# Feed-forward of a decoder kernel: a table of slots for its steps, and the output bias inside the down-projection

## The reference

```
h = shift_token(x)                  # second half of the features comes from the token before
h = (h - mean) / sqrt(var + 1e-5) * lg + lb
a, g = split(h @ w1 + b1)           # 682 hidden features each
x = x + (a * gelu(g)) @ w2 + b2
```

## Time and profile before

| | us |
|---|---|
| median of 3 runs | 2443.47 (2440.64 to 2444.36) |
| the profiled execution, its own time | 2433.82 |
| its span, first to last instruction | 2432.2 |
| TensorE busy | 2219.9 (91%) |
| VectorE busy | 1686.4 (69%) |
| ScalarE busy | 1510.4 (62%) |
| GpSimd busy | 1363.0 (56%) |
| mean granted TensorE clock | 0.960 |

### The profile page before, as it was taken

How to read it: one execution, slowest core, us unless ns; L and a number is a source line. 1 busy time by engine, 2 the same in 40 slices (tenths; PEclk the granted TensorE clock), 3 DMA queues, 4 the chain that set the end, 5 groups by cost and what they waited for, 6 DMA issues and landing times. The chain is left out here.

```text
span 2432.2 us, 44944 instructions
## 1 busy us (share of the span) xinstructions
PE 2219.9 (91%) x14670; PEld 1571.3 (65%) x14760; DVE 1686.4 (69%) x3300; ACT 1510.4 (62%) x3450; POOL 1363.0 (56%) x1456
## 2 busy tenths in 40 slices
PE   2899999899999999799999996898899999978887
PEld 2444444444444543478888885787688888866776
DVE  1777888678888886577787774554687777855553
ACT  1277788678878887567776773333577766753332
POOL 3344665333334444767777664553677676646665
PEclk6699999899999999899999998999999999999998
DMA  8656677656676674110000001000100000001111
GB/s 181 95 106 128 130 145 143 123 137 150 146 159 160 150 149 137 49 47 1 2 1 1 1 6 57 10 9 1 38 1 2 1 2 1 1 22 36 44 39 35
DMA packets 92405, 161.06 MB, mean 66 GB/s; under 512 B 15848, under 2 KB 35032, under 8 KB 92184
## 3 DMA queue, kind: packets, MB, share of 16 engines
q1 hardware_dynamic: 89624, 149.80, 27.7%
q0 software_dynamic: 2560, 8.39, 1.0%
HBM read 93.54 MB, written 59.24 MB: 63 GB/s over the span
## 5 line engine op out<-in xcount | busy, mean ns | idle before, releaser
L923 DVE TENSOR_REDUCE MX<-PS 128x1 f32<-128x512 f32 x1024 | 642.9, 683 | 193.4 <-PE PS L525 183.1
L775 ACT ACTIVATE PT<-PS 128x512 f32<-128x512 f32 x1024 | 545.8, 600 | 132.0 <-PE PS L542 130.2
L525 PE MATMUL PS<-KS,QS 48*128 48x512 f32 x1024 | 355.6, 454 | 56.1 <-DMA KS<-hs 44.1
L542 PE MATMUL PS<-QS,KS 50*128 50x512 f32 x1024 | 385.1, 456 | 6.4 <-ACT PT L775 6.0
L542 PEld LDWEIGHTS PS<-QS,KS 50*128 50x128 f32 x1024 | 164.7, 187 | 269.5 <-issue 212.6
L558 PE MATMUL PS<-PT,VP 128*17 128x512 f32 x2048 | 272.8, 605 | 3.2 <-ACT OT L782 3.1
L628 PE MATMUL PS<-kT,qT 128*128 128x256 f32 (+1 forms) x1536 | 253.7, 306 | 1.6 <-DVE kT L1030 1.6
L525 PEld LDWEIGHTS PS<-KS,QS 48*128 48x128 f32 x1024 | 171.4, 192 | 119.5 <-issue 60.2
L1290 POOL TENSOR_TENSOR PB<-PB,RC 128x512 f32<-128x512 f32 (+1 forms) x256 | 235.0, 935 | 13.3 <-DVE RC L1048 13.3
L847 ACT ACTIVATE PB<-PS,NMf 128x256 f32<-128x256 f32 (+1 forms) x512 | 223.7, 450 | 24.6 <-DVE NMf L1039 22.6
L1272 POOL TENSOR_TENSOR RI<-RI,mhalf 128x8 f32<-128x8 f32 x128 | 213.9, 1671 | 10.7
(11 more groups left out here) (164 smaller groups left out, 5292.3 us busy)
## 6 DMA issues: line engine op xcount, KB each, us to landing
hs<-HL SPq DMA_DIRECT2D x64, 512.0 KB, 3.8
QS<-hs SPq DMA_DIRECT2D x192, 128.0 KB, 6.1
KS<-hs SPq DMA_DIRECT2D x192, 128.0 KB, 8.4
od<-OT SPq DMA_DIRECT2D x64, 256.0 KB, 5.9
OC<-od SPq DMA_DIRECT2D x32, 256.0 KB
cst<-rs SPq DMA_DIRECT2D x32, 256.0 KB
X<-x SPq DMA_DIRECT2D x8, 512.0 KB, 8.6
tab<-ctxT SPq DMA_DIRECT2D x8, 512.0 KB, 7.2
```

The lines of the kernel that those rows point to most:

```text
L525: pe.matmul(PS[:, bank, :], QS[rows, s, h // 2, qt * P:(qt + 1) * P], KS[rows, s, h // 2, :], start=True, stop=True).then_inc(fills("amax" ...
L542: pe.matmul(PS[:, bank, :], KS[rows, s, pair, kt * P:(kt + 1) * P], QS[rows, s, pair, :], start=True, stop=True).then_inc(fills("score", v ...
L775: act.activation(PT[:, kt % 2, 2 * i + half], PS[:, TURNS["score", vb, g, kt, half, i][0], :], ACT.Exp).then_inc(drains("score", vb, g, kt ...
L923: dve.tensor_reduce(MX[:, vb % 2, h // 8, qt, c:c + 1], PS[:, TURNS["amax", vb, h, qt][0], :], AX, ALU.max).then_inc(drains("amax", vb, h, ...
```

## The change

The order of a feed-forward step comes from a table, `MLP_ORDER`: in each of six slots it lists stages with a delay k, and step n issues the stage for batch n-k. A negative delay means that a stage is issued ahead of its batch. Stages that were whole are cut: `mstat` and `mnorm` into halves (two token tiles; half of the features), and the closing normalisation of layer 1 leaves `mdown` and becomes `fstat`, `frstd`, `fnorm`, `fstore`. The load of `Y` is a stage `yload` of its own.

The affine step of `mtr` moves from VectorE to ScalarE, ahead of its copy there:

```
-                dve.tensor_scalar(TT[:], PS[:, bank, :], cols[:, L, 12 + half:13 + half], cols[:, L, 14 + half:15 + half],
-                                  ALU.mult, ALU.add).then_inc(drains("mtr", L, b, half), 1)
+                act.activation(TT[:], PS[:, bank, :], ACT.Identity, bias=cols[:, L, 14 + half:15 + half],
+                               scale=cols[:, L, 12 + half:13 + half]).then_inc(drains("mtr", L, b, half), 1)
```

```
+            def mones(L):
+                dve.memset(U5[32:64], 1.0).then_inc(sem["u_ones"], 1)
...
             def mres(L, b):
-                if L == 0 and b == 0:
-                    pool.wait_ge(sem["b2_in"], 16)
-                pool.wait_ge(sem["hn"], NB * L + b + 1)
-                for i in range(4):
-                    m = pool.tensor_tensor(X[:, b, i], X[:, b, i], b2[:, L], ALU.add)
...
+                pool.wait_ge(sem["y_in"], 16 * (b + 1))
+                pool.wait_ge(sem["hn"], 2 * (NB * L + b) + 2)
                 for i in range(4):
+                    m = pool.tensor_tensor(X[:, b, i], X[:, b, i], Y[:, i], ALU.add)
+                m.then_inc(sem["x_res"], 1)
```

More of the change, by code:

```diff
@@ L156, in window_stages @@
         if n == NU + last - 1:
-            out += [("mstat", L, 0), ("mnorm", L, 0)]
+            out += [("mstat", L, 0, 0), ("mstat", L, 0, 1), ("mnorm", L, 0, 0), ("mnorm", L, 0, 1)]
         for place, (kind, part, k) in enumerate(WINDOW_ORDER):
@@ L218, in all_stages @@
     out += window_stages(0, 6 * [([], [])] + [([("split_mlp", 0, k)], [("split_mlp_lo", 0, k)]) for k in range(14)])
-    out += [("load_rot",), ("rot", 1), ("load_qkv", 1)]
-    out += mlp_stages(0, [[("split_qkv", 1, k)] for k in range(10)])
+    out += [("load_rot",), ("rot", 1)]
+    out += mlp_stages(0, [[("load_qkv", 1, 2 * k), ("load_qkv", 1, 2 * k + 1)] for k in range(5)] + [[("split_qkv", 1, k)] for k in range(10)])
     out += [("load_mlp", 1)]
@@ L666, in mtr @@
             def mtr(L, b, half):
-                pe.wait_ge(sem["hn"], NB * L + b + 1)
+                pe.wait_ge(sem["hn"], 2 * (NB * L + b) + half + 1)
                 bank = vacant(pe, "mtr", L, b, half)
@@ L880, in mup @@
                     act.wait_ge(*filled("mup", L, b, c))
-                    gate, bias, done = PS[64:P, 2 * q, :], cols[64:P, L, 10:11], sem["gate5"]
+                    gate, bias, done = PS[64:126, 2 * q, :], cols[64:126, L, 10:11], sem["gate5"]
                 if c >= 2:
@@ L1079, in mstat, with mnorm @@
                 m.then_inc(sem["mmean"], 1)
-            def mnorm(L, b):
+            def mnorm(L, b, half):
                 s = b % 2
                 T = ST[:, s]
-                dve.wait_ge(sem["mrstd"], NB * L + b + 1)
-                if b >= 2:
-                    dve.wait_ge(*filled("mtr", L, b - 2, 1))
-                for half in range(2):
-                    for i in range(4):
-                        m = dve.tensor_scalar(HN[:, s, i, half * P:(half + 1) * P], XS[:, s, i] if half else X[:, b, i, 0:P],
-                                              T[:, 64 + 2 * i:65 + 2 * i], T[:, 80 + i:81 + i], ALU.subtract, ALU.mult)
-                m.then_inc(sem["hn"], 1)
@@ L1103, in mup @@
+                for i in range(4):
+                    m = dve.tensor_scalar(HN[:, s, i, half * P:(half + 1) * P], XS[:, s, i] if half else X[:, b, i, 0:P],
+                                          T[:, 64 + 2 * i:65 + 2 * i], T[:, 80 + i:81 + i], ALU.subtract, ALU.mult)
+                m.then_inc(sem["hn"], 1)
             def mup(L, b, c):
-                q, n, w = c % 2, P if c < 5 else 64, c if c < 5 else 10
+                q, n, w = c % 2, P if c < 5 else 62, c if c < 5 else 10
                 if c < 5:
@@ new lines, in fstat @@
+            def fstat(L, b, half):
+                T, n = LNF[:, half], 2 * b + half
+                dve.wait_ge(*drained("mdown", L, b, 2 * half))
+                dve.wait_ge(*drained("mdown", L, b, 2 * half + 1))
+                for k in range(2):
+                    dve.bn_stats(T[:, 6 * k:6 * k + 6], X[:, b, 2 * half + k]).then_inc(sem["fstats"], 1)
+                for k in range(2):
+                    dve.wait_ge(sem["fstats"], 2 * n + k + 1)
+                    m = dve.bn_aggr(T[:, 32 + 2 * k:34 + 2 * k], T[:, 6 * k:6 * k + 6])
+                m.then_inc(sem["fmean"], 1)
@@ L1154, in vector, with fnorm @@
+            def fnorm(L, b, half):
+                T = LNF[:, half]
+                dve.wait_ge(sem["frstd"], 2 * b + half + 1)
+                for k in range(2):
+                    x = X[:, b, 2 * half + k]
+                    m = dve.tensor_scalar(x, x, T[:, 32 + 2 * k:33 + 2 * k], T[:, 48 + k:49 + k], ALU.subtract, ALU.mult)
+                m.then_inc(sem["fnormed"], 1)
             does = dict(begin=begin, split_w=split_w, tr_lo=tr_lo, amax=amax, fold=fold, inv=inv, res=res, stats=stats, norm_last=norm_last, window_consts=window_consts, rot=rotations, split_qkv=split_qkv, wzero=wzero,
@@ L1339, in gpsimd, with fstore @@
+            def fstore(L, b, half):
+                pool.wait_ge(sem["fnormed"], 2 * b + half + 1)
+                pool.dma_start(t["out"][b, 2 * half * P:2 * (half + 1) * P].rearrange("(t p) d -> p t d", p=P),
+                               X[:, b, 2 * half:2 * half + 2]).then_inc(sem["out"], 16)
             does = dict(begin=begin, split_w=split_w, mix=mix, mix_sum=mix_sum, heads_lo=heads_lo, ctx_lo=ctx_lo, maxrows=maxrows, scale=scale,
                         out_lo=out_lo, rstd=rstd, norm=norm, add_bo=add_bo,
-                        split_qkv=split_qkv, split_mlp_lo=split_mlp_lo, wpad=wpad, wrn=wrn, wqn=wqn, wscale=wscale, mstat=mstat, mtr=mtr, mup=mup, mres=mres, mdown=mdown,
+                        split_qkv=split_qkv, split_mlp_lo=split_mlp_lo, wpad=wpad, wrn=wrn, wqn=wqn, wscale=wscale, mstat=mstat, mtr=mtr, mup=mup, mres=mres, frstd=frstd, fstore=fstore,
@@ L1458, in load_qkv @@
                         heads_written(sp, NV - 1, 0, tile)
-                for k in range(10):
+                for k in range(10) if piece is None else (piece,):
                     _, _, raw, src = qkv_source(k)
```

171 lines of the change are left out of this document (67 added, 104 removed).

## The result

| | us |
|---|---|
| the changed kernel, median of 4 runs | 2365.23 (2364.60 to 2371.15) |
| the kernel before, beside it, 4 runs | 2443.91 (2440.64 to 2445.07) |
| ratio, 95% interval | 0.9686 (0.9667 to 0.9704) |
| the profiled execution after, own time; span | 2371.15; 2369.3 |

The change made the kernel faster by 78.7 us by the medians. By the two profiled executions the gain is 62.7.

A forecast was written before the change was run, and what follows sets the result against it. TensorE sets the pace in both feed-forward stretches but waits for `HN` and `HT` through orders, not loads. Savings 4.3 + 4.1 + 11.8 + 0.3 + 7.9 + 24.0 + 1.5 = 53.9 us, scaled to 54.1, gave 2389.5; range 2376 to 2408.

The forecast's parts named there:

- A stall of 1.2 is left: 167.1 + 7 x 1.2: Layer 1, steps 1 to 7: late tail stalls TensorE 1.2 us a step before the down-projection; 175.5 in all, 24.0 saved.
- Profiled time 2379.9; runs 2443.47 - 54.1 = 2389.4: Whole kernel: saving of 53.9 us taken from the profiled execution, scaled by 1.004 and taken from the runs' median.
- (a): Rival: VectorE is early enough, no tail stall in either layer; 3.0 + 8.4 us less, 2378; chance 0.13.
- Lead-in, 4.3 and 0.3 predicted: Before each layer's first product: affine pass on ScalarE, 0.69 us each, saves 4.3 in layer 0, 0.3 in layer 1.
- Layer 0, 15.9 predicted: Layer 0's steps: waits for `HN` and `HT` go, saving 4.1 us in step 0 and 11.8 in steps 1 to 7.
- in which TensorE never waits takes 24.0 us: Length of a feed-forward step without waits, from layer 0: transposes 25.29 us apart with a stall of 1.30.
- except where a weight split holds GpSimd in slot 5 (some 4 steps, 0.75 each): 3.0: Layer 0, steps 1 to 7: weight splits on GpSimd make the tail late, adding 3.0 us to 167.1.
- Layer 1, 31.9 predicted: Layer 1's steps: waits for `HN` and `HT` go, saving 7.9 us in step 0 and 24.0 in steps 1 to 7.
- (b): Rival: port holds add 2.8 us to the tail in each layer 1 step, step 28.0; +19.6, 2409; chance 0.18.
- (c): Rival: affine Identity pass between gate functions forces four ScalarE table loads a step; +21 us, 2410; chance 0.02.
- (d): Rival: slower than before, each VectorE two-port operation in layer 1 held a full 1.3 us pass; step 34.4, 2454; chance 0.03.
- (e): Rival: a queued wait, such as GpSimd's stores for the closing norm, hands back each gain; 2443 us; chance 0.02.

The follow-up runs named there:

- stat3: The changed kernel with both halves of the statistics of batch n+2 and the adds of `Y` moved to the end of slot 3; median 2364.19 us, ratio 0.9675.

## Why the prediction was right, and where it was wrong

The direction, the mechanism and the order of the parts were right: the waits for `HN` and `HT` were made by orders, and they went. The time was not, for two separate reasons. Of the steps of the sum, "A stall of 1.2 is left: 167.1 + 7 x 1.2" failed most, by its size: the stall is 0.52 to 0.57 in five steps and nothing in two. And the step from the profile to the median failed.

*The conversion from the profile to the median failed, 15.5 of the 24.3 us.* The prediction took "Profiled time 2379.9; runs 2443.47 - 54.1 = 2389.4", that is 9.6 between them. Measured, the median lies 5.9 below its profiled execution. Both are draws from a spread that the three runs of before (2440.64 to 2444.36) did not show, and that 50 more runs put at 29 us (whether the first chip has less of it, as its four runs of after within 6.6 us suggest, or this was chance, stays open). The range ended at 2376, "under (a) by 2"; it had no term for this. The other medians of the same or an equal feed-forward are 2376.45, 2385.46 and 2368.72: the first two lie in the range, the third 7.3 below it. Had the 9.6 held, the median would have been 2380.8, in the range with the sum as wrong as it is; had the sum been right and the draw the same, it would have been about 2375.5, just outside. So how far the median lies outside the range is for the larger part the luck of the draw.

(The rest of the 24.3 is 8.8: the 10.3 below and the 2.6 of "between", less the 3.9 of "ahead" and 0.2 of rounding and of what lies outside the span.)

*The sum was 10.3 too small.* What came true is nearer rival (a), fed fully, given 0.13: its 53.9 + 11.4 = 65.3 stands beside the measured 64.2. That is partly luck: a stall is left in layer 1, and the fed step is shorter than (a) had it. By the prediction's steps:

1. Lead-in, 4.3 and 0.3 predicted, 4.0 and 0.15 measured. The path was right (copies, `TT` single). Each affine pass took 0.78, not 0.69 (timelines of ScalarE and GpSimd):

```profile
1481.00 0.78 ACT L877 ACTIVATE TT<-PS,cols 128x512 f32<-128x512 f32 x1 [8.02 <-PE PS L672]
1481.81 0.62 ACT L882 CAST HT<-TT 128x512 fp32r<-128x512 f32 x1
1483.93 0.78 ACT L877 ACTIVATE TT<-PS,cols 128x512 f32<-128x512 f32 x1 [1.50 <-POOL HT L1319]
```
```profile
1482.57 1.26 POOL L1319 TENSOR_TENSOR HT<-TT,HT 128x512 fp32r<-128x512 f32 x1 [5.42 <-ACT HT L882]
1485.43 1.26 POOL L1319 TENSOR_TENSOR HT<-TT,HT 128x512 fp32r<-128x512 f32 x1 [1.60 <-ACT HT L882]
```

2. Layer 0, 15.9 predicted, 20.05 measured. Step 0 takes 19.05 (1486.80 to 1505.85) where 18.8 was put down, so nothing of the miss is there. Steps 1 to 7 take 165.70 where 170.1 was put down, for two reasons. The first is the fed step, "in which TensorE never waits takes 24.0 us". It takes 23.75, and step 7 takes 23.03 for 23.1. The 24.0 was one step of the earlier trace rows less its wait of 1.30, and such a step holds some 0.2 more behind the wait. This is worth 1.6 us in each layer. The second is "except where a weight split holds GpSimd in slot 5 (some 4 steps, 0.75 each): 3.0". A split beside the tail does lengthen its second pass (in four steps, to 1.13 or 1.82 for 0.74), but in layer 0, where no closing normalisation and no adds stand ahead, the tail has that much to spare. Steps 1 to 7 take only 0.17 more than fed ones in sum, and TensorE shows no idle time. One of the two longest (VectorE, then GpSimd), where the first down-projection follows at 1535.20:

```profile
1532.57 0.69 DVE L1137 TENSOR_TENSOR UR<-UR 32x512 fp32r<-32x512 f32 x1 [0.29 <-ACT UR L906]
1533.27 1.82 DVE L1138 SCALAR_TENSOR_TENSOR UR<-UR,cols 32x512 fp32r<-32x512 f32 x1
...
1533.26 1.28 POOL L1273 TENSOR_TENSOR WQ<-WQ 128x512 fp32r<-128x512 f32 x1 [3.90 <-ACT WQ L796]
```

3. Layer 1, 31.9 predicted, 38.0 measured. Step 0 takes 18.09 (2157.91 to 2176.00) for 18.4. Steps 1 to 7 take 169.7 for 175.5: 1.6 of it is the fed step, and the rest, 4.2, is "A stall of 1.2 is left: 167.1 + 7 x 1.2", the largest miss. It is there, before the first down-projection group as forecast, but at 0.52 to 0.57 in five steps, 2.7 for 8.4 (the steps of layer 1 are 1.5 longer in sum than the fed ones beyond these waits). Counted as the prediction did (the sixth up-projection ends at 2249.25, 5.6 before the need), the product starts at 1.89 for 2.3, the copies are done at 3.9 for 4.5, the tail at 6.0 for 6.8: each link was put a little too long, and a wait that is the difference of two long sums doubles by it. Steps 1 and 7 have none at all. The bound given, "none", was right as a bound. The cause was right too: the prediction charged the statistics ahead of the product and the blocked tail, and the wait goes when either is taken away.

4. The end, 1.5 predicted, 2.0 in "close". The 2.2 less of idle time (5.38 for 7.59) came as forecast; of the 0.7 that was to be lost behind it, some 0.1 shows. "Between" gained 2.6 that no step had.

The other rivals: (b) is out, as the tail pays 0.67 and not 2.8 for its neighbour in the steps with the wait (0.95 in step 7, which has none). (c) is out, with one table load in a layer as before (groups by line of the changed kernel):

```profile
L896 ACT ACT_TABLE_LOAD x2 | 2.6, 1283 | 0.0
```

By the Trainium skill, ScalarE: Activation LUTs, Table sets, identity is in every set; the trace agrees. (d) needed every `HN` half held for a whole pass. The second half of `HN` did get longer, 0.562 for 0.335 in the mean of an operation (the first 0.498 for 0.594), but either half is early enough. (e) is out, as no gain was handed back.

On the rule of the shared port (the Trainium skill, Advanced Engine Details and Errata, Mode Summary), the trace agrees for `HN` and goes further than that section: the tail's passes, which have two tensors as sources, are longer beside GpSimd's adds too, 0.98 to 1.28 for 0.68 and 1.12 for 0.74. The rule was weighed in the prediction as a danger to the change (a 1.3 at the product's neighbours), and what it is worth here is the 0.5 us in a step that moving GpSimd's adds by two slots gives back.

## What to carry to other kernels

Where no queue is full and TensorE still waits, change the order first: the table brought 59 of 67 us, and the bias as ones, worth 23.6 alone, little beside it, because both removed the same wait. The wait before the down-projection shows the same: it was made of two terms, and taking either away removed all of it, so that one run alone would have called the other term harmless. Before a range is drawn from the spread of three runs, ask what else varies between executions. Compare the stretch that was changed, cut at rows of the trace, and not the whole: it repeats to 0.6 us where the median moves by 20. Take the length of a fed step from a step without any wait: one less its wait was 0.25 too long, and seven of them made 1.6. And an add on GpSimd that nobody waits for isn't free if it lies beside a VectorE pass that somebody does wait for.

## What the runs showed of the hardware

The granted clock between 900 and 1100 us differs between executions of the same code from 0.80 to 0.96, and the time with it. Steps with a stall of 2.0 to 2.3 us have a clock of 0.94 in some cases, for 1.5 us more, and steps with one of 0.52 keep 1.00; the kernel before has 1.00 in a step with two waits of 2 (29.41 us), so the stall alone doesn't decide it. Nor does the lower clock always cost time: a neighbouring step of the kernel before has 0.94 and is as long, since its waits shrink instead (1.64 for `HN` where the other has 2.32, and none before the down-projection where the other has 0.61). The two steps in the windows view:

```profile
2235.36:2264.76 29.40, 25.76 (x138) 21.64 (x138) 16.96 (x46) 9.61 (x15) 19.10 (x24) 0.94 0.13 45
2264.76:2294.17 29.41, 24.48 (x139) 20.44 (x139) 17.01 (x46) 9.52 (x15) 19.09 (x24) 1.00 0.13 45
```

A lower clock once stands elsewhere: in `stat3`, from 40 us behind the end of layer 0's run, the clock is 0.76 for 20 us where the changed kernel has 1.00, and "between" is 483.1 for 479.6, which hides what `stat3` gained in its "rest":

```profile
1701.36:1721.36 20.00, 18.39 (x105) 15.50 (x105) 12.94 (x25) 12.06 (x37) 11.22 (x13) 0.76 0.01 1
```
```profile
1711.55:1731.55 20.00, 17.46 (x123) 14.61 (x124) 16.39 (x32) 14.96 (x45) 13.51 (x16) 1.00 0.01 1
```

A ScalarE pass of 128x512 from PSUM takes 0.776 with a column for the bias and one for the scale (mean of 32), and 0.689 with a bias column alone.
